# Perceiver block on one core: bias rows ahead of the eighth weight unit, earlier splits of the hidden layer, and the first norm on ScalarE

## The reference

```python
x = x + _L0_xattn_ref(_layernorm(x), ctx_1024, Wq, bq, Wkv, bkv, Wproj, bproj)   # 16 heads of 32
x = x + _L0_attn_ref(_layernorm(x), WQ, WK, WV_down, WV_up)                      # 16 heads of 64
x = x + _L0_ffn_ref(_layernorm(x), Wg, bg, W1, b1, W2, b2)                       # 8 experts, top 2

# the experts
gates = jax.nn.softmax(x @ Wg + bg, axis=-1)
_, top_idx = jax.lax.top_k(gates, K)                       # K = 2 of E = 8
h = jnp.einsum('btd,edh->bteh', x, W1) + b1[None, None]    # D = 512, H = 2048
h = jax.nn.gelu(h, approximate=False)
eo = jnp.einsum('bteh,ehd->bted', h, W2) + b2[None, None]
return jnp.einsum('bte,bted->btd', g, eo)
```

## Time and profile before

| | |
|---|---|
| three timed runs | 1398.45, 1401.89, 1401.93 us, median 1401.89 |
| the profiled execution | 1393.57 us; span 1391.8 us |
| TensorE busy | 1325.6 us, 95% of the span |
| VectorE, ScalarE, GpSimd busy | 67%, 55%, 7% |
| granted TensorE clock, mean | 0.989 of full speed |
| DMA | 145.11 MB, mean 104 GB/s |

### The profile page before, as it was taken

One profiled execution on the slowest core, in us unless ns is written; L12 is line 12 of the kernel. 1 busy time (PEld: TensorE's weight loads), 2 busy tenths in 40 slices (PEclk: granted clock), 3 DMA queues, 4 the chain that ended last, 5 costly groups with the idle time before them and its releaser, 6 DMA issues.

```text
span 1391.8 us, 22065 instructions
## 1 busy us (share of the span) xinstructions
PE 1325.6 (95%) x7439; PEld 1149.9 (83%) x7440; DVE 937.9 (67%) x1512; ACT 760.0 (55%) x1327; POOL 101.6 (7%) x84
## 2 busy tenths in 40 slices
PE   7999999999999999999999999987899699999997
PEld 5898988888889898888889989976677587877776
DVE  6566666666667666666666766758488856487884
ACT  5465555565555555555556554654332526477772
POOL 0000000000000000000000000044452120000002
PEclk9999999999999999999999999999899899999999
DMA  5211121011111112101111010472538457399993
GB/s 196 95 54 32 30 52 43 26 45 35 44 30 38 30 34 60 30 26 45 45 34 45 23 39 27 82 156 71 94 112 307 149 197 255 112 349 333 342 346 106
DMA packets 126852, 145.11 MB, mean 104 GB/s; under 512 B 64072, under 2 KB 67528, under 8 KB 126800
## 3 DMA queue, kind: packets, MB, share of 16 engines
q1 hardware_dynamic: 125536, 140.44, 32.6%
q0 software_dynamic: 1280, 4.20, 0.9%
HBM read 124.75 MB, written 19.86 MB: 104 GB/s over the span
## 4 chain that ended last, share of the span: by engine, by line
PE 71%; DVE 13%; issue 6%; DMA 4%; ACT 4%; SPq 1%; DVEq 0%; POOL 0%; ACTq 0%
PE ps_scores L151 12%; PE ps_scores L153 12%; PE ps_scores L152 12%; PE ps_out L819 6%; PE ps_turn L807 5%; PE ps_scores L796 5%; PE ps_turn L694 2%; DMA wu_raw<-in_L_ffn_W_dram 2%; PE ps_scores L2116 2%; PE ps_scores L2114 2%; PE ps_scores L2115 2%; DVE stat L619 2%; DVE Ks L539 2%; ACT wu_hi L1823 1%; DVE wu_lo L2005 1%
## 5 line engine op out<-in xcount | busy, mean ns | idle before, releaser
L539 DVE SCALAR_TENSOR_TENSOR Ks<-ps_scores,bkc,Ks 64x384 fp32r<-64x384 f32 (+2 forms) x254 | 160.6, 632 | 143.4 <-ACT Ks L416 140.8
L151 PE MATMUL ps_scores<-cT_hi,Wkv_hi 128*128 128x384 f32 (+2 forms) x504 | 181.9, 361 | 0.0
L501 ACT ACTIVATE Pr<-ps_scores,stat 128x705 f32<-128x705 f32 (+1 forms) x128 | 119.5, 934 | 110.0 <-DVE stat L619 110.0
L153 PE MATMUL ps_scores<-cT_hi,Wkv_lo 128*128 128x384 f32 (+2 forms) x504 | 172.9, 343 | 0.0
L152 PE MATMUL ps_scores<-cT_lo,Wkv_hi 128*128 128x384 f32 (+2 forms) x504 | 172.4, 342 | 0.0
L416 ACT ACTIVATE Ks<-ps_scores,bkc 64x384 fp32r<-64x384 f32 (+2 forms) x254 | 149.4, 588 | 39.1 <-PE ps_scores L153 35.5
L545 DVE TENSOR_TENSOR Vs<-ps_scores,Vs 128x512 fp32r<-128x512 f32 (+1 forms) x103 | 71.2, 691 | 147.0 <-ACT Vs L420 146.4
L151 PE MATMUL ps_scores<-Wkv_hi,cT_hi 128*128 128x512 f32 (+1 forms) x412 | 169.9, 412 | 0.0
L488 ACT CAST PT<-ps_turn 128x512 fp32r<-128x512 f32 (+2 forms) x256 | 110.2, 483 | 102.4 <-PE ps_turn L807 101.5
L153 PE MATMUL ps_scores<-Wkv_hi,cT_lo 128*128 128x512 f32 (+1 forms) x412 | 161.8, 393 | 0.0
L152 PE MATMUL ps_scores<-Wkv_lo,cT_hi 128*128 128x512 f32 (+1 forms) x412 | 161.1, 391 | 0.0
(11 more groups left out here) (383 smaller groups left out, 2466.8 us busy)
## 6 DMA issues: line engine op xcount, KB each, us to landing
wu_raw<-in_L_ffn_W_dram SPq DMA_DIRECT2D x64, 1024.0 KB, 7.4
raw<-in_ctx_dram SPq DMA_DIRECT2D x16, 768.0 KB, 4.6
raw<-in_ctx_dram SPq DMA_DIRECT2D x8, 1024.0 KB, 5.4
raw<-in_ctx_dram SPq DMA_DIRECT2D x8, 512.0 KB
sorted_x<-zeros SPq DMA_DIRECT2D x1, 4096.0 KB, 14.9
sorted_out<-zeros SPq DMA_DIRECT2D x1, 4096.0 KB, 25.4
o_heads<-U SPq DMA_DIRECT2D x56, 64.0 KB, 1.7
oA<-o_heads SPq DMA_DIRECT2D x8, 448.0 KB, 9.4
```

The costliest lines, as they stand in the source:

```text
L151: nc.tensor.matmul(out_ap, sh, mh, start=(i == 0), stop=False)
L153: last = nc.tensor.matmul(out_ap, sl, mh, start=False, stop=(i == len(pairs) - 1))
L501: nc.scalar.activation(Pr[:, i % 2, 0:VALID[c]], S_cols(c, 0, VALID[c], 0 if ctx else i % 2), ACT.Exp, bias=stat[:, 0, c, i:i + 1], accum_ ...
L539: ins = nc.vector.scalar_tensor_tensor(out=Ks[c][64:128, j, o:o + wide], in0=acc[64 * h:64 * h + 64, 0:wide], scalar=bkc[:, j:j + 1], in1= ...
```

## The change

Four edits, each of them only an order or an engine.

1. The first norm. DVE computes mean, root and now also `shift` = −mean · root (`shift=` of `norm_vector`), and stops there. ScalarE applies the norm: four activations `Identity` with `shift` as bias and the root as scale, behind `first_kv_hi(5)`.
2. The four turns of the tokens go behind projection piece 7, together; `x_hi` and `x_lo` follow as four in a row, ahead of the evacuation of piece 7.
3. `Wq_lo` goes from DVE to GpSimd, behind the memsets of the start.
4. In the experts' tiles, `hidden_hi(3)` and `hidden_lo(3)` go ahead of unit 4, the next tile's tokens (`gathered_hi`, `gathered_lo`) ahead of unit 5, and SyncE loads the bias rows ahead of unit 7, behind units 4 to 6.

```diff
@@ norm_vector
+            if shift is not None:
+                nc.vector.scalar_tensor_tensor(out=shift[:, g], in0=mv[:, g, 0], scalar=-1.0, in1=rs[:, g],
+                                               op0=ALU.mult, op1=ALU.mult).then_inc(sem("ln_scaled"), 1)
+                return
             for t in tiles:
                 ins = nc.vector.tensor_scalar(xn[:, t, :], x[:, t, :], mv[:, t, 0:1], rs[:, t:t + 1],
                                               ALU.subtract, ALU.mult)
@@ GpSimd, behind the memsets of the start
+                pool.wait_ge(sem("wq_hi"), 1)
+                pool.wait_ge(sem("ln_scaled"), 1)
+                nc.gpsimd.tensor_tensor(Wq_lo[:, :, :], Wq_raw[:, :, :], f32(Wq_hi[:, :, :]), ALU.subtract) \
+                    .then_inc(sem("wq_lo"), 1)
@@ ScalarE, opening
                 first_kv_hi(5)
-                x_hi(0)
-                x_hi(1)
+                act.wait_ge(sem("ln_scaled"), 1)
+                for t in range(TT):
+                    ins = nc.scalar.activation(x_tok[:, t, :], x_tok[:, t, :], ACT.Identity,
+                                               bias=shift1[:, t:t + 1], scale=lnt1[4][:, t:t + 1])
+                ins.then_inc(sem("ln_done"), 1)
                 first_kv_hi(6)
-                x_hi(2)
-                x_hi(3)
+                for k in range(KC):
+                    x_hi(k)
                 first_kv_hi(7)
@@ DVE, opening
                 first_kv_lo(5)
-                x_lo(0)
-                x_lo(1)
-                dve.wait_ge(sem("wq_hi"), 1)
-                nc.vector.tensor_tensor(Wq_lo[:, :, :], Wq_raw[:, :, :], f32(Wq_hi[:, :, :]), ALU.subtract) \
-                    .then_inc(sem("wq_lo"), 1)
                 first_kv_lo(6)
-                x_lo(2)
-                x_lo(3)
+                for k in range(KC):
+                    x_lo(k)
                 first_kv_lo(7)
@@ TensorE, opening
-                    if n == 5:
-                        turn_x(0)
-                        turn_x(1)
-                    elif n == 6:
-                        turn_x(2)
-                        turn_x(3)
-                    elif n == 7:
+                    if n == 7:
+                        for k in range(KC):
+                            turn_x(k)
@@ SyncE, changing tile
                     for v in range(RING, UNITS):
+                        if v == UNITS - 1:
+                            sp.wait_ge(sem("l1_made"), t * QT + QT)
+                            load_b1(e + 1)
                         load_next(e + 1, v)
-                    sp.wait_ge(sem("l1_made"), t * QT + QT)
-                    load_b1(e + 1)
@@ ScalarE, tile
                 hidden_hi(2)
-                unit_hi(4)
                 hidden_hi(3)
-                unit_hi(5)
                 if final:
                     return
+                unit_hi(4)
                 gathered_hi(t + 1)
+                unit_hi(5)
                 unit_hi(6)
@@ DVE, tile
                 hidden_lo(2)
-                unit_lo(4)
                 hidden_lo(3)
-                unit_lo(5)
...
                 else:
+                    unit_lo(4)
                     gathered_lo(t + 1)
+                    unit_lo(5)
```

More of the change, by code:

```diff
@@ L102, in perceiver_kernel, with norm_vector @@
         EARLY, LATE, END = 512, 79520, 212640
-        def norm_vector(dve, n, x, xn, tmp, tiles=range(TT), prepare=None, between=None):
+        def norm_vector(dve, n, x, xn, tmp, tiles=range(TT), prepare=None, between=None, shift=None):
             done = sem("ln_step")
@@ L135, in norm_vector @@
             link(nc.vector.tensor_tensor(rs[:, g], rs[:, g], root[:, g], ALU.mult))
+            assert at[0] == 7 * n
+            if shift is not None:
+                nc.vector.scalar_tensor_tensor(out=shift[:, g], in0=mv[:, g, 0], scalar=-1.0, in1=rs[:, g],
+                                               op0=ALU.mult, op1=ALU.mult).then_inc(sem("ln_scaled"), 1)
+                return
             for t in tiles:
@@ L139, in norm_vector @@
             ins.then_inc(sem("ln_done"), 1)
-            assert at[0] == 7 * n
         def norm_scalar(act, n, tmp, tiles=range(TT)):
@@ L203, in perceiver_kernel @@
                 early("rt1", [P, TT]), early("rs1", [P, TT]))
+        shift1 = early("shift1", [P, TT])
         bkc = early("bkc", [64, NP])
@@ L573, in _ @@
                 dve.wait_ge(sem("x_in"), 16)
-                norm_vector(dve, 1, x_tok, x_tok, lnt1, between=lambda: first_kv_lo(3))
+                norm_vector(dve, 1, x_tok, x_tok, lnt1, between=lambda: first_kv_lo(3), shift=shift1)
                 def x_lo(k):
```

## The result

The changed kernel takes 1391.45 us (median of 6 runs, 1388.39 to 1394.79), the kernel before 1399.35 (6 runs, 1397.47 to 1401.93) beside it: a ratio of 0.9945, 95% interval 0.9928 to 0.9962, or 7.7 us less (5.3 to 10.1). 1396.9 was predicted, with 1393.5 as the low end.

The account below looks back on a forecast made before the run. TensorE was taken to hang on the weight stream, near its own limit, through three in-order queues. Terms −1.3 − 0.7 − 3.0 = −5.0 from the median 1401.89 gave 1396.9 us, range 1393.5 to 1402.0.

Parts of the forecast that it names:

- The opening, −1.3: Opening: token turns behind projection pieces 6 and 7 let the query projection start at 37.5 instead of 38.76, 1.3 us less.
- The granted clock needs no term: TensorE's clock: 1.00 throughout in the tiles, the opening's pace taken as it is across the hole; no us allowed.
- First expert, −0.7: First expert's tile start: bias rows land one transfer earlier, so it starts at 1171.65 instead of 1172.35, 0.7 us less.
- Only the edits together do this: Expert tiles: a tile starts at 1274.5 instead of 1277.22 only with all edits, since each wait alone is covered by the other.
- Five tiles, −3.0: Five tiles between 1223.38 and 1357.42: TensorE moves forward against the weight stream by one transfer, once; 3.0 us less taken.
- The upper bound of 4.5: Five expert tiles: most they could gain at TensorE's own busy time, 129.5 us instead of 134.04, 4.5 less.
- the 25.9: Expert tiles: TensorE's own busy time, taken as about 25.9 us a tile.
- The rival in which TensorE becomes the bound again: Expert tiles: DMA holes close and all five tiles go at 25.9; −6.5 in all, 1395.4; chance 0.17.
- The slower rival: Expert tiles: a hole in the weight stream between unit 7 and the next unit 0; +7.0 in all, 1408.9; chance 0.10.
- the wait behind a late unit 3: Expert tiles, a sign of being wrong: layer 2's third quarter waits for `h_lo` behind a late unit 3; no size given.

Follow-up runs that it names:

- x_opening: The three edits of the opening alone, on the kernel before; ratio 0.9988 to the kernel before.
- x_h3_b1: Kernel before with bias rows ahead of unit 7 and `hidden(3)` ahead of unit 4, gathered tokens still behind unit 5; ratio 1.0031 to the kernel before.
- x_more4: Changed kernel plus four 256 KB transfers in each tile that loads weights, each waiting for the one before to land; ratio 1.0162 to the kernel before.
- x_more4d: Changed kernel plus four 256 KB transfers a tile into DRAM, each with its own place and no wait for the one before; ratio 0.9970 to the kernel before.
- x_order: Kernel before with only `hidden(3)` ahead of unit 4 and gathered tokens ahead of unit 5, bias rows where they were; ratio 0.9991 to the kernel before.

## Why the prediction was off

1. **The opening, −1.3.** Right in its steps: turns in one block at 33.28 (33.6 said), ScalarE's norm 2.94 us (2.5 to 4.0), GpSimd 4.63 (4.73), projection at 37.43 (37.5). What failed is the sentence "The granted clock needs no term". In half of the traces the hole of 2.9 us left TensorE at the lower clock behind it. The start of the projection is late by 1.5, 1.5 and 2.7 us then, over six traces 0.9 on average, so this part is worth about 2.2 rather than 1.3; `x_opening` timed 1.7, in an interval that just takes in no gain (ratio up to 1.0002).
2. **First expert, −0.7.** The mechanism was right and the size was not. The prediction took the wait from one trace, and that trace had the smallest. Over three traces with the old order the first four tiles take 102.7, 104.3 and 104.1, with the new one 101.9: −1.8. And it was not the first expert's alone: the second expert's last tile, which waited for nothing in the prediction's trace, is followed by waits for the bias rows of 0.34 and 0.90 us in the other two.
3. **"Only the edits together do this."** Right: 135.09 and 136.19 apart, 129.3 together; two of the three without the gathered tokens' place, 136.97.
4. **Five tiles, −3.0.** This is the step that failed: "Hence the weight stream hardly moves, and TensorE moves forward against it by one transfer, about 2.7 us, once, not per tile." The stream did move, with the tiles, because it was not at its limit: the engines moved 377 to 394 GB/s when asked to. What held it back was when its loads were issued. SyncE waited for DVE's splits 38 times in these five tiles of the kernel before, 83.8 us in all, and the splits stand in in-order queues. How much of the gain this wait alone is worth was not tried (with more buffers, say). Over three traces with the old order and six with the new, the five tiles take 134.4 and 130.2 on average, −4.2, and −4.8 in the two traces first compared. The upper bound of 4.5 was about right, the value inside it was chosen by the wrong argument. Nor was the 25.9 behind that bound TensorE's own time: the busy time of these tiles fell with the waits, from 25.9 to 26.0 down to 25.5 to 25.7. The rival in which TensorE becomes the bound again had the mechanism, and the Trainium skill's figure had spoken for it.
5. **The slower rival** (a hole between unit 7 and the next unit 0) did not show: the share stayed at 0.98 to 1.03. Its kin did, where one more split stood ahead of the tile's input (`x_h3_b1`). Of the prediction's signs of being wrong one came, the wait behind a late unit 3, and it cost one tile 1.3 us.
6. **The base.** The terms as measured sum to 2.2 + 1.8 + 4.2 = 8.2, which lies in the interval of the 7.7 that was timed. The sum was made against a trace whose nine tiles (236.76) were the shortest of three and whose opening had the full clock, so most of what it lacked was not in it to be read. And the three runs of the kernel before had a median of 1401.89, six had 1399.35: that is 2.5 of the 5.5 us between 1396.9 and 1391.45. In ratios the prediction was 0.9964 with a low end of 0.9940, and 0.9945 lies inside.

## What to carry to other kernels

A DMA busy share of 1.00 doesn't say that the stream is at its limit; ask whether its loads are issued late, behind what frees their buffers, and test it with a few bytes more. When two waits cover each other, count the third one too: the edits of a stage can gain 4 us together and cost as much when one of them is left out. A wait of 2 us can cost more than its length, since the clock may fall behind it. And before work is given to GpSimd, look at what VectorE runs beside it on SBUF, however small: a 0.17 us step ahead of a critical path took 4.5 us.

## What the runs showed of the hardware

- A VectorE `tensor_scalar` on 128x4 in SBUF stood still for the whole of GpSimd's `tensor_tensor` (4.53 us), twice of two, and a `tensor_tensor` on 128x1 with both operands in SBUF for the rest of one (2.2 to 2.4 us instead of 0.16), in every trace; a `tensor_scalar` on 128x1 that reads one column of another tile did not (0.15). Splits of `Vs` with an operand in PSUM were not slowed (0.69).
- In the opening the granted clock of TensorE fell to half behind an idle stretch of 2.9 us in three of six executions of the same code, behind 3.85 and 5.61 us in both, and behind 1.26 or less in none of nine. In the experts' tiles it fell behind 1.83 to 2.27 us (four times in `x_more4`, once each in `x_more4d` and `x_order`), and not behind 2.38 and 2.80 (`x_more4`).
- The DMA busy share goes beyond 1: 1.05 at 394 GB/s in a tile, 1.06 at 406 in one microsecond, and 1.00 at anything from 343 (`x_order`) to 361.
- Two traces of one kernel differ by 2 us over nine tiles and by 2.7 at the query projection. One trace sizes a wait no better than that.
